# One set of 23 expert tiles in place of two sets of 13 and 17, with row slots given in three parts

## What is computed

```python
x = x + attention(layernorm(x), ctx_1024)          # 16 heads, 77 keys
flat = layernorm(x).reshape(T, D)                  # T = 1024, D = 128
probs = softmax(flat @ router_w.T)
topk_p, topk_i = top_k(probs, 2)
topk_w = topk_p / topk_p.sum(-1, keepdims=True)
combine = zeros((T, 8)).at[arange(T)[:, None], topk_i].add(topk_w)
out = 0
for e in range(8):
    out = out + _mlp(flat, w_fc[e], w_proj[e]) * combine[:, e:e + 1]
out = out + _mlp(flat, shared_fc, shared_proj)
x = x + out
```

## Time and profile before

| | |
|---|---|
| median of 3 runs | 144.6 us (144.14 to 144.84) |
| the profiled execution | 144.31 us |
| its span | 142.3 us, 3074 instructions |
| TensorE busy in the span | 129.0 us (91%) |
| first product on an expert tile (L1226) | at 72.97 us |
| end of the last `down` of an expert tile | at 129.7 us |

### The profile page before, as it was taken

One profiled execution on the slowest core, in us unless ns is written; L12 is line 12 of the kernel. 1 busy time (PEld: TensorE's weight loads), 2 busy tenths in 40 slices (PEclk: granted clock), 3 DMA queues, 4 the chain that ended last, 5 costly groups with the idle time before them and its releaser, 6 DMA issues.

```text
span 142.3 us, 3074 instructions
## 1 busy us (share of the span) xinstructions
PE 129.0 (91%) x1041; PEld 110.8 (78%) x1042; DVE 83.1 (58%) x218; ACT 74.6 (52%) x154; POOL 78.3 (55%) x125
## 2 busy tenths in 40 slices
PE   6997798988988898988999999999999999999940
PEld 2543677786885878764899999999999999996730
DVE  0669998697788879267658343332333333631633
ACT  3126637595674748637436565555555565554400
POOL 4285795020211657683017878877787887866300
PEclk9999999999999999999999999999999999999995
DMA  4845595479530001016959511695778616600252
GB/s 108 232 172 200 119 292 168 150 194 266 172 139 0 5 0 38 19 57 172 271 199 267 180 58 38 162 342 209 235 252 276 184 37 178 230 20 5 9 176 92
DMA packets 15246, 21.08 MB, mean 148 GB/s; under 512 B 1890, under 2 KB 11238, under 8 KB 15232
## 3 DMA queue, kind: packets, MB, share of 16 engines
q1 hardware_dynamic: 13184, 18.28, 44.1%
q0 software_dynamic: 1472, 2.14, 4.5%
q10 hardware_dynamic: 576, 0.47, 1.0%
HBM read 16.20 MB, written 5.60 MB: 153 GB/s over the span
## 4 chain that ended last, share of the span: by engine, by line
PE 74%; DVE 6%; issue 5%; ACT 4%; POOL 4%; DMA 4%; POOLq 0%; ACTq 0%; DVEq 0%
PE ps L1226 19%; PE ps L1239 19%; PE ps L1077 9%; PE ps L1061 5%; PE ps L973 4%; PE ps L1049 4%; PE ps L1043 3%; ACT p_area L574 3%; PE ps L1182 3%; DMA g_area<-y_dram 3%; PE ps L1211 2%; POOL slots_dram L529 2%; DVE s_max L751 2%; DVE p_area L759 2%; DMA y_dram<-x_area,g_area 2%
## 5 line engine op out<-in xcount | busy, mean ns | idle before, releaser
L909 DVE TENSOR_TENSOR hid<-n_area 128x512 f32<-128x512 f32 x38 | 26.3, 693 | 35.4 <-ACT n_area L640 35.1
L543 POOL DMA_INDIRECT y_dram<-x_area,g_area x30 | 34.6, 1154 | 10.3 <-issue 6.9
L640 ACT ACTIVATE n_area<-ps 128x512 f32<-128x512 f32 x38 | 22.6, 596 | 18.8 <-PE ps L1226 17.0
L529 POOL DMA_INDIRECT slots_dram<-rows,slot x16 | 17.1, 1068 | 12.7 <-DVE rows L825 7.3
L1077 PE MATMUL ps<-v_area,p_area 128*128 128x72 f32 x160 | 19.0, 273 | 0.0
L1077 PEld LDWEIGHTS ps<-v_area,p_area 128*128 128x128 f32 x160 | 18.6, 192 | 0.0
L1239 PE MATMUL ps<-w,hid 128*128 128x128 f32 x128 | 16.9, 275 | 0.0
L1226 PE MATMUL ps<-v_area,w 128*128 128x128 f32 x128 | 16.7, 276 | 0.0
L656 ACT ACTIVATE x_area<-ps,g_area 128x128 f32<-128x128 f32 x30 | 11.0, 368 | 8.9 <-PE ps L1239 8.9
L1239 PEld LDWEIGHTS ps<-w,hid 128*128 128x128 f32 x128 | 15.6, 192 | 0.0
L1226 PEld LDWEIGHTS ps<-v_area,w 128*128 128x128 f32 x128 | 15.4, 192 | 0.0
(11 more groups left out here) (149 smaller groups left out, 173.5 us busy)
## 6 DMA issues: line engine op xcount, KB each, us to landing
p_area<-w_all SPq DMA_DIRECT2D x14, 512.0 KB, 3.9
w<-w_all SPq DMA_DIRECT2D x9, 512.0 KB, 3.9
g_area<-slots_dram SPq DMA_DIRECT2D x7, 264.0 KB, 3.6
slots_dram<-empty SPq DMA_DIRECT2D x1, 1122.0 KB, 8.6
slots_dram<-empty SPq DMA_DIRECT2D x1, 858.0 KB, 8.5
x_area<-x SPq DMA_DIRECT2D x2, 256.0 KB, 3.4
y_dram<-x_area,g_area POOLq DMA_INDIRECT x30
g_area<-y_dram SPq DMA_DIRECT2D x2, 192.0 KB, 3.1
```

What stands on the lines that cost most here:

```text
L529: pool.indirect_dma_start(out=slots_dram, out_offset=bass.IndirectOffsetOnAxis(ap=slot[:, k, q:q + 1], axis=0), in_=rows[:, q, k, :], in_o ...
L543: pool.indirect_dma_start(out=y_dram, out_offset=bass.IndirectOffsetOnAxis(ap=xg[:, i, ID:ID + 1].bitcast(U32), axis=0), in_=y_sb[:, i % Y ...
L640: act.activation(r[:, u % RSLOTS, :], ps[:, UP_BANK[u % UPBANKS], :], ACT.Relu).then_inc(relu_done, 1)
L909: dve.tensor_tensor(hid[:, u % HSLOTS, :], r[:, u % RSLOTS, :], r[:, u % RSLOTS, :], ALU.mult)\
```

## The change

There is one set of expert tiles for all tokens: 8 + 15 = 23 tiles (`NTILE`), with one extra of each possible kind counted once. All 16 row scatters land in it, so no tile can be read back before the last of them. The slots are given in three parts, `SETS = ((0, 3), (3, 5), (5, NT))`. Since a part's counts aren't known when the ones ahead of it are given, each part takes its extra tiles behind those taken before, and if an expert has begun one that isn't full, its rows go on in that one (`now`, `full_at`, `step_to`, `next_less`, `rest`: small arithmetic on 8 experts). The first part's share of it is 8 more instructions on POOL (`first_next`), the second part's 7 on DVE (`next_set`). Which expert an extra tile belongs to is worked out at the end for all parts together (`nets` three times and `all_nets`, 13 instructions, with `end_of(2)` 14).

In POOL's queue the row scatters of the first part stand between the last `root_inverse2`, and those of token tiles 3 and 4 behind them: ten of sixteen stand ahead of what needs the last top experts. SP loads the weights of the first four extra tiles (`AHEAD`) ahead of the row groups. The shared expert's second half goes ahead of the expert tiles, followed by 14 `keep_warm` products (`IDLE`). The results come back and are added in two halves of 4 token tiles at the very end, 1 MB in four loads of 256 KB.

```diff
-SETS = ((0, 3), (3, NT))
+SETS = ((0, 3), (3, 5), (5, NT))
+EXTRA = TOPK * NT - 1
+NTILE = NE + EXTRA
...
+AHEAD = 4
+IDLE = 14
...
             eng.wait_ge(y_out, 16 * NTILE)
+            eng.dma_start(y_in[:, k, b * TB:(b + 1) * TB, :], rows_of(y_dram[k * B * S:(k + 1) * B * S, :])[:, b, :, :])\
+               .then_inc(y_in_done[b], 16)
...
+            sp.wait_ge(net_done, 1)
+            for j in range(AHEAD):
+                load_extra(j)
             slots_v = slots_dram.rearrange("(i p) c -> p i c", p=P)
+            sp.wait_ge(slots_done, 16 * TOPK * NT)
+            for g, (i, count) in enumerate(GROUPS):
+                sp.dma_start(xg[:, i:i + count, :], slots_v[:, i:i + count, :]).then_inc(xg_in[g], 16)
+            for j in range(AHEAD, EXTRA):
+                load_extra(j)
...
+            first_next()
+            root_inverse2(split + 2)
             send_rows(0, 0)
-            root_inverse2(split + 2)
             send_rows(0, 1)
-            send_rows(0, 2)
             root_inverse2(split + 3)
+            send_row(0, 2, 0)
             root_inverse2(split + 4)
-            for q in range(split, NT):
-                send_rows(1, q)
+            send_row(0, 2, 1)
+            for b, (first, last) in enumerate(SETS):
+                for q in range(first, last):
+                    if b > 0:
+                        send_rows(b, q)
...
+            read_ranks(1)
+            count_extra(1)
+            place_extra(1)
             residual(NT - 2)
             residual_stats(NT - 2)
             attention_out(NT - 1)
             top_of(NT - 3)
-            square(0)
+            slots_by_expert(1)
+            assign(1)
             residual(NT - 1)
             residual_stats(NT - 1)
+            weigh(1)
+            square(0)
             square(1)
             top_of(NT - 2)
+            next_set(1)
             square(2)
             top_of(NT - 1)
-            route(1)
+            route(2)
             square(3)
+            read_ranks(2)
+            count_extra(2)
+            place_extra(2)
+            slots_by_expert(2)
+            assign(2)
+            weigh(2)
+            end_of(2)
+            for b in range(NS):
+                nets(b)
+            all_nets()
+            add_shared(0)
+            for u in range(FT, 2 * FT):
+                square(u)
+            add_shared(1)
+            for i in range(NTILE):
+                square(block_of(i))
...
-            down_shared(0, 1)
-            ranks(1)
-            down_shared(1, 2)
+            down_shared(0, 0, 1)
+            ranks(2)
+            down_shared(0, 1, FT)
+            up_shared(1, 0, FT)
+            down_shared(1, 0, FT)
+            pe.wait_ge(top_read, NT - 1)
+            keep_warm(IDLE)
             transpose_group(0)
-            down_shared(2, FT)
             up(0)
             up(1)
```

More of the change, by code:

```diff
@@ L40 @@
 SMALL = 3 * HD
-SETS = ((0, 3), (3, NT))
-EXTRA = tuple(TOPK * (last - first) - 1 for first, last in SETS)
-TILES = tuple(NE + n for n in EXTRA)
-TILE0 = (0, TILES[0])
-EXTRA0 = (0, EXTRA[0])
-NTILE = sum(TILES)
-NEXTRA = sum(EXTRA)
-MAXEXTRA = max(EXTRA)
+SETS = ((0, 3), (3, 5), (5, NT))
+NS = len(SETS)
+EXTRA = TOPK * NT - 1
+NTILE = NE + EXTRA
 MAXSET = max(last - first for first, last in SETS)
@@ new lines, in end_of, with next_set @@
+            def end_of(b):
+                link(dve.tensor_tensor(ends[:, b, :], extra[:, b, :], base_tile[:, b, :], ALU.add))
+            def next_set(b):
+                link(dve.tensor_tensor(is_new[:, :], extra[:, b, :], extra[:, b - 1, :], ALU.is_gt))
+                link(dve.tensor_tensor(is_new[:, :], is_new[:, :], step_to[:, :], ALU.mult))
+                link(dve.tensor_tensor(now[:, :], now[:, :], is_new[:, :], ALU.add))
+                step(dve.tensor_scalar(full_at[:, :], extra[:, b, :], float(P), float(P), ALU.mult, ALU.add))
+                end_of(b)
+                link(dve.tensor_tensor(rest[:, b, :], ends[:, b, NE - 1:NE].broadcast_to([P, NE]), ends[:, b, :],
+                                       ALU.subtract))
+                link(dve.tensor_tensor(next_less[:, :], rest[:, b, :], now[:, :], ALU.subtract))
@@ L872, in nets @@
-                with nc.allow_low_precision("whole numbers below eight"):
-                    dve.tensor_reduce(tile_net[:, b, 0:n], tile_cmp[:, 0:n, :], AX_X, ALU.add).then_inc(net_done, 1)
+                    dve.wait_ge(next_ready, 1)
+                    end = ends[0:1, 0, :]
+                else:
+                    link(dve.tensor_tensor(tile_end[:, :], ends[0:1, b, :], rest[0:1, b - 1, :], ALU.add))
+                    end = tile_end[:, :]
+                link(dve.tensor_tensor(tile_cmp[:, :, :], end.unsqueeze(1).broadcast_to([1, EXTRA, NE]),
+                                       iota_tile[0:1, :].unsqueeze(2).broadcast_to([1, EXTRA, NE]), ALU.is_le))
@@ L962, in _ @@
-            add_shared(TB, half, NTILE + 2)
-            add_shared(half, NT, NTILE + 3)
-            add_terms(1, SETS[0][1], half, 2)
-            add_terms(1, half, NT, 3)
+            read_ranks(2)
[9 more added lines that the diff above has]
+            add_shared(0)
+            for u in range(FT, 2 * FT):
+                square(u)
@@ new lines, in _ @@
+            add_shared(1)
+            for i in range(NTILE):
+                square(block_of(i))
+            dve.wait_ge(base_done, B)
+            for b in range(B):
+                dve.wait_ge(y_in_done[b], 16 * TOPK)
+                tiles = slice(b * TB, (b + 1) * TB)
+                link(dve.tensor_tensor(x2[:, tiles, :], x2[:, tiles, :], y_in[:, 0, tiles, :], ALU.add))
+                dve.tensor_tensor(x2[:, tiles, :], x2[:, tiles, :], y_in[:, 1, tiles, :], ALU.add)\
+                   .then_inc(total_done, 1)
```

336 lines of the change are left out of this document (151 added, 185 removed).

## The result

The change makes the kernel slower: 156.79 us, median of four runs (155.59 to 158.09), against 144.4 (144.14 to 144.84), a ratio of 1.083 with the 95% interval [1.079, 1.087]. The forecast was 150.7 and its range ended at 153.8: the sign was right, the size was not. The profiled execution took 155.59 with a span of 153.8, so 4.9 us have to be found against it; the median lies 1.2 above it.

What follows compares the result with a forecast made beforehand. PE, busy 91%, was taken as the bound. First `up` at 91.3, tiles 43.4 and clock 0.9 gave 135.6 against 129.7, +5.9; tail +0.5 made +6.4 on 144.31, so 150.7 us, range 147.0 to 153.8.

Steps and rivals of the forecast that it cites:

- a break-even start of 86.3: Start of the expert tiles on PE: with the tail kept, the change breaks even if the first `up` starts at 86.3 us.

Runs made afterwards that it cites:

- e10: e9 reordered on DVE and PE (first half's squares later, residual of token tile 7 and last ranks earlier), 8 unused products: 147.32 us, 1.019 of before.
- e5: e4 with the last six row scatters left out and not waited for, y_dram zeroed early, no unused products: 144.6 us, 1.001 of before.
- e2: Changed kernel with no extra weight loads ahead of the row groups (AHEAD 0 for 4): 151.76 us, 1.049 of before.
- e3: Changed kernel with up to three extra weight loads under way in place of two: 154.16 us, no ratio given.
- e7: e4 with two extra weight loads ahead of the row groups in place of none: 149.18 us, 1.035 of before.
- e1: Changed kernel with 36 unused products in place of 14 ahead of the tiles: 155.66 us, 1.074 of before.
- e4: Changed kernel with no extra loads ahead, three loads under way and 22 unused products: 149.2 us, 1.032 of before.
- e8: e4 with one shared-expert square on DVE, square(2), moved behind the last top experts: 149.93 us, 1.041 of before.
- e11: e10 without the unused products (8 become 0): 145.84 us, 1.011 of before.
- e9: e4 with the four squares of the shared expert's second half reading one factor from PSUM, 16 unused products: 148.96 us, 1.033 of before.

## What to carry to other kernels

If a chain of loads has a place for each only when an older one is done, compare its pitch (a landing plus the issuing, over the number under way) with the consumer's, and give the difference a term of its own: 2.54 against 1.79 cost 2.8 us at the end of the stretch. Don't let loads of half a megabyte be under way when a small transfer is sent on whose landing the next stage waits, and price a small transfer's landing by what will be under way, not by a quiet row. And saving work on the bound engine counts only from when its input is there: here 13.3 us less work started 20.1 us later, and one subtraction (a break-even start of 86.3) told most versions apart.

## What the runs showed of the hardware

- A POOL row scatter takes 0.96 us alone, up to 1.48 beside one VectorE square of 128x512 with both inputs in SBUF, and 2.78 beside four in a row. With one input in PSUM it takes 0.96. A small POOL instruction behaves likewise: the one of L398 took 0.97 beside squares and 0.29 in e10, where none ran. The squares lose nothing, four take 2.48 with a scatter beside them and in e5 without.
- A row scatter lands 1.33 to 1.39 us behind its record's end, and 3.0 to 5.0 when loads of 512 KB were under way, then 0.2 to 0.4 behind the landing of the last one issued before its record ended.
- In the changed kernel the granted clock fell in the middle of the program too, 3.1 us after PE's last product, and it was back in the stretch 95 to 97, with PE at work since 91.23. A wait of 2.19 dropped it in three profiled executions (e2, e3, e7) and left it up in three (changed, e1, e4); one of 2.63 left it up in e8, and those of 2.82 in e10 and e11 and of 3.06 in e9 dropped it. Unused products hold it up, but they stand in PE's queue: the last 8 of them cost 1.5 us once the rows were there before them (147.32 to 145.84).
